# A second landing buffer for the first weight loads, new orders on all five engines, and 94 identity products in the first two pairs

## The reference

```python
x = x + (x @ W0[subject]^T + b0[subject])                      # 512 -> 512
h = relu(x @ W1[language] + b1[language])                       # 512 -> 128
x = x + layernorm(x + h @ W2[language] + b2[language]) * gamma[language] + beta[language]
ctx = causal_ema(x, tau_ctx)                                    # along the 128 steps
gated = x * sigmoid([x, ctx] @ Wg^T + bg)
mod = 0.5 + sigmoid(gelu(x @ Wn1^T + bn1) @ wn2^T + bn2)        # 32 factors per step
traces[d] = causal_ema(gated * mod[d], tau[d]);  temporal = sum_d traces[d] * softmax(blend)[d]
gate = sigmoid(temporal @ Wtemp^T + btemp);  soma = gelu(x @ Wsoma^T + bsoma)
x = x + layernorm((soma * gate) @ Wout^T) * gamma2 + beta2
x = x + zX * laplace_x(x) + zY * laplace_y(x) + zR * x * (1 - x)
```

## Time and profile before

| | |
|---|---|
| Median of three runs | 1017.53 us (1014.01 to 1021.61) |
| Profiled execution, its span | 1015.61 us, 1013.9 us |
| TensorE busy | 905.2 us (89%), 6088 products |
| VectorE busy | 803.3 us (79%) |
| GpSimd busy | 574.8 us (57%) |
| ScalarE busy | 399.1 us (39%) |
| Data moved by DMA | 133.28 MB, mean 131 GB/s |

### The profile page before, as it was taken

How to read it: one execution, slowest core, us unless ns; L and a number is a source line. 1 busy time by engine, 2 the same in 40 slices (tenths; PEclk the granted TensorE clock), 3 DMA queues, 4 the chain that set the end, 5 groups by cost and what they waited for, 6 DMA issues and landing times.

```text
span 1013.9 us, 18886 instructions
## 1 busy us (share of the span) xinstructions
PE 905.2 (89%) x6088; PEld 768.6 (76%) x6088; DVE 803.3 (79%) x1333; ACT 399.1 (39%) x730; POOL 574.8 (57%) x654
## 2 busy tenths in 40 slices
PE   2459999999999999999999999999999999998961
PEld 1338697888878797888979797988878797887740
DVE  4757879787987978797988979787988979786862
ACT  3464433434343442434343442534343442424220
POOL 1234627475665658475665658475665658563533
PEclk9869999999999999999999999999999999999995
DMA  6773344444434444434444444444444444421011
GB/s 225 226 240 104 104 130 131 126 138 143 136 126 145 140 142 143 139 129 153 136 126 146 142 147 145 129 137 145 135 126 146 136 143 126 127 74 32 32 42 62
DMA packets 92815, 133.28 MB, mean 131 GB/s; under 512 B 15692, under 2 KB 32588, under 8 KB 92716
## 3 DMA queue, kind: packets, MB, share of 16 engines
q1 hardware_dynamic: 88372, 125.93, 40.0%
q10 hardware_dynamic: 4344, 6.14, 1.8%
HBM read 106.86 MB, written 8.39 MB: 114 GB/s over the span
## 4 chain that ended last, share of the span: by engine, by line
DVE 32%; POOL 20%; PE 15%; issue 13%; SPq 8%; DMA 7%; ACT 4%; ACTq 1%; POOLq 0%; DVEq 0%
POOL work L417 11%; PE bank L1249 7%; DMA w_land<-in_L_cond_weight 6%; DVE w_r L831 6%; SPq L312 6%; DVE work L1009 4%; DVE work L931 3%; PE bank L1241 2%; DVE work L1016 2%; POOL work L458 2%; DVE work L1027 2%; ACT w_r L541 2%; POOL work L433 2%; PE bank L1234 2%; POOL work L447 2%
## 5 line engine op out<-in xcount | busy, mean ns | idle before, releaser
L417 POOL TENSOR_TENSOR work<-work 128x448 f32<-128x448 f32 (+3 forms) x224 | 190.9, 852 | 32.3 <-DVE work L1000 13.0
L1249 PE MATMUL bank<-x2h,wg_r 128*128 128x256 f32 x1536 | 195.9, 284 | 5.8 <-DVE bank L948 3.6
L1249 PEld LDWEIGHTS bank<-x2h,wg_r 128*128 128x128 f32 x1536 | 185.1, 189 | 17.4 <-issue 7.8
L1000 DVE TENSOR_TENSOR work<-bank,work 128x512 f32<-128x512 f32 (+7 forms) x256 | 105.7, 449 | 43.1 <-POOL work L417 21.6
L831 DVE TENSOR_TENSOR w_r<-w_land,w_r 128x1024 fp32r<-128x1024 f32 x64 | 79.0, 1235 | 45.7 <-ACT w_r L541 45.7
L1379 PE MATMUL bank<-gh,amath 128*128 128x512 f32 x384 | 105.8, 412 | 8.0 <-DVE amath L977 5.0
L433 POOL TENSOR_TENSOR work<-work 128x512 f32<-128x512 f32 x32 | 44.9, 1403 | 118.8 <-DMA work<-in_L_cond_beta 110.8
L1241 PE MATMUL bank<-w_r,xh 128*128 128x512 f32 x384 | 103.5, 414 | 9.2 <-DVE w_r L831 6.5
L1241 PE MATMUL bank<-wout_r,th 128*128 128x512 f32 x384 | 99.1, 408 | 5.2 <-DVE th L1032 3.3
L541 ACT ACTIVATE w_r<-w_land 128x1024 fp32r<-128x1024 f32 x64 | 67.7, 1057 | 87.2 <-DMA w_land<-in_L_cond_weight 80.1
L1249 PE MATMUL bank<-x2h,wsoma_r 128*128 128x256 f32 x768 | 99.4, 286 | 0.0
(11 more groups left out here) (142 smaller groups left out, 1605.1 us busy)
## 6 DMA issues: line engine op xcount, KB each, us to landing
w_land<-in_L_cond_weight SPq DMA_DIRECT2D x64, 512.0 KB, 3.8
w_t<-in_L_cond_W SPq DMA_DIRECT2D x64, 256.0 KB, 3.6
work<-work SPq DMA_DIRECT2D x64, 224.0 KB, 2.5
work<-in_xT SPq DMA_DIRECT2D x32, 256.0 KB, 3.8
b_t<-in_L_cond_bias SPq DMA_DIRECT2D x32, 256.0 KB, 4.1
work<-in_x SPq DMA_DIRECT2D x32, 256.0 KB, 3.8
gamma_t<-in_L_cond_gamma SPq DMA_DIRECT2D x32, 256.0 KB, 3.4
work<-in_L_cond_beta SPq DMA_DIRECT2D x32, 256.0 KB, 3.4
```

The source lines that it names most:

```text
L417: g_.tensor_tensor(dst, dst, src, ALU.add).then_inc(S["acc_ready"], 1)
L1000: ins = v_.tensor_tensor(dst, src, g_q[:, 2 * half:2 * half + 2, :, 0:width], ALU.mult)
L1249: ins = mm(dst, weight[:, w_part, first_block + a, o * P:(o + 1) * P], act[:, x_part, a], start=(not onto and a + w_part + x_part == 0), s ...
```

## The change

1. **Second landing buffer.** The upper half of `x2b`, which no pair uses before pair 1, becomes `spare_land`. For the first three rows (b = 0, 1, 2) the second half of the weight lands there, so that both halves can be in flight. From b = 3 on all is as before. The semaphore of a landed half is split in two, one for each half. `x2_plus_beta(1, r)` on GpSimd waits until the spare buffer has been read.
2. **New orders.** The lists of all five engines are written in another order, and the turn of the loop is cut at another place. `beta2`, `gamma2` and the three z vectors are loaded late, on SP's queue (`late_constants`); before, beta2 and gamma2 were on ScalarE's queue at the very start. `logs`, `exps`, `exponents`, the softmax, `vj` and the matrices' parts also move.
3. **Identity products.** `idle_products(n)` issues n products of the 128 x 128 identity with itself into bank 5, which nobody reads. It stands at ten places of TensorE's list, 10, 5, 18, 12, 5, 11 and 10 in the turn i = -2 and 9, 6 and 8 in the turn i = -1: 94 in all. None stands in a later turn.

```diff
+        spare_land = buf("x2b")[:, CC // 2 * C:].rearrange("p (a c) -> p a c", a=CC // 2)
...
+        SPARE_ROWS = 3
+        def landing(b, half):
+            if b < SPARE_ROWS:
+                return (spare_land, 2 * b) if half else (w0_land[:, :, :], max(0, 2 * b - 1))
+            return w0_land[:, :, :], 2 * b - 1 if (b == SPARE_ROWS and not half) else 2 * b + half
...
                 def load_w0(p, r, half):
                     b = 2 * p + r
-                    if half or b:
-                        sp.wait_ge(S["w0hi_ready"], 2 * b + half)
-                        sp.wait_ge(S["w0lo_ready"], 2 * b + half)
+                    land, n_free = landing(b, half)
+                    if n_free:
+                        sp.wait_ge(S["w0hi_ready"], n_free)
+                        sp.wait_ge(S["w0lo_ready"], n_free)
...
+                def late_constants():
+                    sp.dma_start(beta2[:, :], l2_beta.partition_broadcast(P)).then_inc(beta2_loaded, 16)
+                    sp.dma_start(gamma2[:, :], l2_gamma.partition_broadcast(P)).then_inc(gamma2_loaded, 16)
+                    for dst, src in ((zraw[:, 0], zx), (zraw[:, 1], zy), (zraw[:, 2], zr)):
+                        sp.dma_start(dst, src.partition_broadcast(P)).then_inc(const2_loaded, 16)
...
+            def idle_products(n):
+                for _ in range(n):
+                    mm(bank[5][:, 0:P], ident[:, :], ident[:, :], start=True, stop=True)
...
                 if live(i + 2):
                     adapter(i + 2, 0)
+                if i == -1:
+                    idle_products(8)
...
+                if i == -2:
+                    idle_products(18)
                 if live(i + 2):
                     l0(i + 2, 1, FRONT)
```

More of the change, by code:

```diff
@@ L802, in _ @@
                     slopes(i - 1, 1)
+                if live(i + 1):
+                    wg_tanh(i + 1, 1)
+                if i == -2:
+                    vj_hi_parts(range(Q))
+                if live(i + 3):
+                    x_hi(i + 3, 0)
+                if i == -1:
+                    act.wait_ge(lo_made, 4 * CC)
+                if live(i + 1):
+                    soma_gelu(i + 1, 0)
                 if live(i + 3):
                     w0_hi(i + 3, 0, 0)
-                if i == -8:
-                    load_matrix(0)
                 if live(i + 1):
-                    wg_tanh(i + 1, 1)
+                    soma_gelu(i + 1, 1)
+                if i == -1:
+                    next_matrix(4)
+                if i == -2:
+                    mod_weights()
+                if live(i + 1):
+                    wg_tanh(i + 1, 2)
+                    wg_tanh(i + 1, 3)
+                if live(i + 2):
+                    x1_turned(i + 2, 1)
+                if live(i + 1):
+                    mod_rows(i + 1)
+                    amat_hi(i + 1, 0)
+                if live(i + 2):
+                    relu(i + 2, 1)
+                if i == -1:
+                    hi_parts(4)
+                if live(i + 1):
+                    soma_gelu(i + 1, 2)
+                if i == -3:
+                    exps()
+                if live(i + 1):
+                    g_hi(i + 1, 0)
+                if i == -2:
+                    next_matrix(3)
         @block.vector
@@ L1074, in _ @@
             for i in STEPS:
+                if live(i - 1):
+                    out_centred(i - 1, 1)
+                if i == 1:
+                    dve.wait_ge(zt_ready, 1)
+                if live(i - 1):
+                    final_sum(i - 1, 0)
+                if live(i + 1):
+                    x2_lo(i + 1, 1)
+                if live(i + 2):
+                    x1_row(i + 2, 0)
+                if live(i):
+                    temporal(i, 0)
+                if i == -1:
+                    vj_lo_parts(range(Q))
@@ new lines, in _ @@
+                if live(i - 1):
+                    final(i - 1, 0)
+                if live(i):
+                    temporal(i, 1)
+                    temporal_lo(i, 0)
+                    temporal_lo(i, 1)
+                if i == -2:
+                    decays()
+                if live(i - 1):
+                    x3_row(i - 1, 1)
+                if live(i + 2):
+                    w0_lo(i + 2, 1, 0)
+                if live(i + 1):
+                    ctx_sums(i + 1, 0)
+                if live(i):
+                    soma_gate(i, 0)
+                    soma_gate(i, 1)
@@ L1421, in _ @@
             for i in STEPS:
+                if i == -1:
+                    idle_products(9)
+                if live(i + 1):
+                    x2_turn(i + 1, 1)
+                if live(i):
+                    state(i, 1, 3)
+                if live(i + 2):
+                    l0(i + 2, 0, BACK)
+                if live(i):
+                    spread_states(i, 1)
+                if i == -2:
+                    blend_rows()
                 if live(i):
                     tn_turn(i, 0)
+                if i == -2:
+                    idle_products(10)
+                if i == -1:
+                    idle_products(6)
                 if live(i + 2):
@@ L1443, in _ @@
                     gate_part(i, 1)
-                if live(i + 2):
-                    adapter(i + 2, 0)
                 if i == -1:
```

460 lines of the change are left out of this document (204 added, 256 removed).

## The result

The changed kernel takes 1053.85 us (median of four runs, 1048.48 to 1055.47) where the kernel before, beside it on the same chip, takes 1019.07 us: a ratio of 1.0346, 95% interval 1.0294 to 1.0397. I had forecast 993 us, faster. It is 35 us slower, outside my range. The profiled execution took 1048.48 us, with a span of 1046.8 us.

A forecast was written before the change was run, and what follows sets the result against it. It took TensorE to bound the middle, and a chain of loads, splits and small products the start. 1015.6 (profiled execution) - 13 (start) - 10 (middle) = 992.6, so 993 us; range 979 to 1011.

The forecast's parts named there:

- The bound of the middle: Middle pairs: TensorE sets the pace, busy 55.20 of 57.11 us, so at most 1.9 us a pair can be won.
- The middle, -10 us: Pairs from 2 on: the new order removes 0.7 of 1.24 us of named waits over 14 pairs; bounds 0 and -24.
- and the last W0 half behind them on SP follow it: Middle, SP's list: the six shifts and the last W0 half follow `x3_row(1)`, which comes 2 us earlier than 468.67.
- The start, -13 us: Start up to pair 0's middle: spare buffer and earlier loads open it sooner, worth -13 us; bounds -4 and -17.
- The term counted from `gate_x(0, 0)`: Start: products run closed up from `gate_x(0, 0)`, about 64 against 78.1 us before, 14 us, less 1 for lo parts.
- The products, near nothing: Start, TensorE: 94 identity products lie mostly in waits and raise the clock; alone near nothing, bounds -5 to +6 us.
- slower by the middle: Rival, middle: xT lands late behind W0 and b0 on SP, all TensorE waits; at 1.5 us a pair 1025; chance 0.06.
- A reading of the clock: Start: four products like those of `hidden` take 2.08 us at 1.2 GHz, 0.9 us at full clock.

The follow-up runs named there:

- e18: e8 with one step moved on SP: the load of W0's second half of row 1 ahead of the shifts of row 1; 991.79 us, ratio 0.9739.
- e4: The changed kernel with the store of a pair's row 1 moved on SP ahead of the next pair's row 0 shifts; 1036.32 us, ratio 1.0203.
- e14: e4 with the load of W0's second half of row 1 also ahead of the shifts of row 1 on SP; 1026.29 us, ratio 1.0065.
- e8: The kernel before with the second landing buffer alone, all lists in the old order, no identity products; 1014.11 us, ratio 0.9974.
- e17: The changed kernel; on SP, store and W0's second half of row 0 ahead of row 0's shifts, row 1's half ahead of row 1's; 1021.55 us, ratio 1.0023.
- e2: The changed kernel without the 94 identity products; 1056.73 us, ratio 1.0391.
- e15: e8 with 86 identity products added at the same steps of TensorE's list as in the change; 1017.75 us, ratio 1.0000.
- e7: The changed kernel; on SP, row 1's b0 and xT ahead of row 0's W0 load, and the store ahead of row 0's shifts; 1046.98 us, ratio 1.0290.

## Why the prediction was wrong

**The bound of the middle: wrong, and the root.** I read 55.2 of 57.1 us busy and said that at most 1.9 us a pair could be won and that TensorE sets the pace. It was a closed chain of 57.3 us beside an engine that needs 55.5 (e18). I had used the chain view only for two loads at the start. With that reading I took SP's places for cover and thought a shift of queues could cost nothing but what TensorE waits for by name.

**The middle, -10 us: wrong step, measured +31.** I priced what the new lists remove and didn't walk SP's list through one closed pair. What I named did happen: `out_centred(1)` no longer waits for GpSimd, and `x3_row(1)` comes 1 us earlier in the pair (32.1 us behind `mod_turn`, 33.0 before; I had said 2). But the shifts that follow it come later (35.1 against 33.8), since SP is still issuing the store and beta of other rows. My sentence was that the six shifts "and the last W0 half behind them on SP follow it": they didn't, and what the change had put behind shifts (the previous store, at 461.62) I had not listed at all. e4 prices that store at 15 to 17.5 us, e14 the half of row 1 at 10 to 14 more. The latter stands behind the shifts in the old list too, so e14 does not undo the change there, it takes out a link that both kernels have; in the old lists it is worth 22 us (e18 against e8).

**And the rest of the new lists isn't better.** With the links out of both, the new lists take 57.6 us a pair (e17), the old ones 55.5 (e18). The exact step isn't found.

**The start, -13 us: half of it came, and none of it stayed.** `gate_ctx(0, 0)` came at 63.18 us, 13.5 earlier where I had forecast 18; on the way there, `y_row` of row 0 came at 33.53 (forecast 30) and that of row 1 at 49.92 (46). The term counted from `gate_x(0, 0)`, 78.1 to 64, less 1; it opens at 71.45, so that the 14 us were 6.7. SP, ScalarE, TensorE in the changed kernel:

```profile
45.59 0.34 SPq L298 DMA_DIRECT2D b_t<-in_L_cond_b  x1
```

```profile
48.34 0.37 ACT L587 ACTIVATE work<-bank,b_t 128x128 f32<-128x128 f32 x1 [5.12 <-DMA b_t<-in_L_cond_b]
```

```profile
67.54 1.10 PE L1315 MATMUL bank<-w_t,work 128*128 128x512 f32 x2 [2.63 <-DMA w_t<-in_L_cond_W]
68.47 3.33 PE L1439 MATMUL bank<-ident 128*128 128x128 f32 x16
71.45 3.34 PE L1273 MATMUL bank<-x2h,wg_r 128*128 128x256 f32 x24
```

b1 was issued at 45.6 (forecast 41) and `relu` still waits 5.12 us for it; the adapter of row (1, 0) waits for W2, and eight identity products follow at the low clock. The gain is 7.9 us at `mod_turn(0)` and 0.5 at `mod_turn(1)`: I had ended the walk at pair 0 and let the products "run closed up" behind it.

**The products, near nothing: right.** They cost no more than my bounds; in e2 and e15 their worth can't be told from zero. At one place they stand in the way: the eight ahead of `gate_x(0, 0)` run behind a wait, 3.0 us in all, at a granted clock of 0.50 from 69 us on. Without any of the 94 (e2) `mod_turn(0)` comes 2.1 us earlier; that it is these eight is not shown.

**The rival that came nearest** was "slower by the middle" (0.06), with a price of 1.5 us a pair from xT behind W0. The side was right; of the mechanism, only that xT is in the ring: moving it (e7) gave nothing. A closed chain was none of my rivals.

**A reading of the clock.** I put the four products of `hidden` at 31.02 us, 2.08 us, at 1.2 GHz. The column has 1.00 there. The same eight records take 2.08 us at 48.64 us, where the column has 0.50, so the duration bears me out and the column doesn't; its 1.00 in the first 33 us of that trace is not evidence of a full clock. No term of the sum hangs on it.

## What to carry to other kernels

A bounding engine that is busy 97% of a pair can still be waiting on a closed chain; the chain view over one whole period says so, and a wait list, which names only the last wait, doesn't. In an in-order queue, ask of every step that stands behind one which waits for the end of an iteration whether the next iteration needs it: move it ahead if its own operands are there (one load: 22 us here, 24 by the ratios). And an early gain counts only if it is still there one period later.

## What the runs showed of the hardware

- An identity product of 128 x 128 in f32 takes 0.23 us where the clock is up (18 in 4.18 us), and 0.4 us where it is at 0.50 in all but the first third of a us (eight in 3.33 us).
- TensorE's clock came down behind a stretch with waits although it was never idle for long: busy 0.70, 1.11, 1.17 and 1.37 us of each 2 us from 92 to 100 us, and 0.50 from there to 108, through 2.0 us of 2.0 busy between 100 and 102. From 205 to 835 us, with 40 us of named waits in these 630 us, it is granted 1.00.
- Issue alone is a load on a queue: six shifts hold SP for 4.2 us and W0's load follows 5.4 us behind their start, twice a pair; SPq L331 is 11% of the changed kernel's chain.
- The same eight records of plain f32 products take 2.08 us at 31.02 us of the trace before, with a granted clock of 1.00 in the column, and 2.08 at 48.64 with 0.50; where the clock is up they take 1.05 to 1.16. At the start of a trace the duration of a known product can tell the clock where the column doesn't.
